# Message passing with 42-node ranges, batches added in pairs per PSUM bank, one-hots three batches ahead, and VectorE's batch work all ahead of the reset gate

## The reference, cut to what matters

```python
def _gated_graph_conv(x, src, dst, emask, W, wih, whh, bih, bhh):
    h = x
    for i in range(STEPS):                      # 3 steps, and this for each of 3 edge types
        m = h @ W[i]
        msg = m[src] * emask[:, None]
        agg = jax.ops.segment_sum(msg, dst, num_segments=N)
        h = _gru_cell(agg, h, wih, whh, bih, bhh)
    return h
...
dst = (3125 * uniform(50000) ** 2.0).astype(int32); sorted   # dense at low nodes, thin at high ones
```

## Time and profile before

| what | us |
|---|---|
| median of 3 runs | 2778.94 (2778.64 to 2779.45) |
| the profiled execution: span from first to last instruction | 3036.4 |
| three steps of the graph convolution in it (601 to 2500) | 1899 |
| everything ahead of them (mix stage) | 601 |
| everything behind them (expert stage) | 536 |

### The profile page before, as it was taken

One profiled execution on the slowest core, in us unless ns is written; L12 is line 12 of the kernel. 1 busy time (PEld: TensorE's weight loads), 2 busy tenths in 40 slices (PEclk: granted clock), 3 DMA queues, 4 the chain that ended last, 5 costly groups with the idle time before them and its releaser, 6 DMA issues. The chain is left out here.

```text
span 3036.4 us, 39301 instructions
## 1 busy us (share of the span) xinstructions
PE 2646.3 (87%) x13041; PEld 1701.2 (56%) x13041; DVE 1592.0 (52%) x3119; ACT 642.5 (21%) x1180; POOL 1358.7 (45%) x1375
## 2 busy tenths in 40 slices
PE   5898899779988898798899996898888966999997
PEld 3434455465555556554455554654545556788886
DVE  6798777445555554355555552466766784011110
ACT  3211000111111114111111123122212221332232
POOL 0000500066666661666666634666666600333333
PEclk7899999889999999899999998899999985999998
DMA  4300766334444443444444434343444423133223
GB/s 129 132 1 1 286 240 218 117 104 129 144 144 137 138 135 104 126 125 145 128 129 145 145 97 157 118 121 112 123 129 124 122 58 100 35 90 92 65 64 72
DMA packets 201473, 362.85 MB, mean 120 GB/s; under 512 B 27937, under 2 KB 156109, under 8 KB 201104
## 3 DMA queue, kind: packets, MB, share of 16 engines
q0 software_dynamic: 67776, 169.95, 20.2%
q1 hardware_dynamic: 129564, 186.48, 18.4%
q10 hardware_dynamic: 3956, 4.19, 0.5%
HBM read 293.37 MB, written 70.34 MB: 120 GB/s over the span
## 5 line engine op out<-in xcount | busy, mean ns | idle before, releaser
L1453 POOL DMA_INDIRECT xnT<-h_rows,idx x780 | 775.2, 994 | 378.0 <-issue 206.6
L1124 PEld LDWEIGHTS g_pagg<-g_onehot,xnT 128*128 128x128 f16 x4680 | 337.1, 99 | 408.3 <-issue 396.3
L1124 PE MATMUL g_pagg<-g_onehot,xnT 128*128 128x144 f16 x4680 | 416.0, 230 | 154.8 <-issue 152.8
L1295 DVE TENSOR_TENSOR g_agg<-g_agg,g_pagg 128x288 f32 x585 | 265.1, 453 | 370.6 <-remote 159.6
L1453 POOL DMA_INDIRECT xnT<-xn_rows,idx x366 | 360.6, 985 | 198.8 <-issue 95.0
L1298 DVE SCALAR_TENSOR_TENSOR g_onehot<-iota_keys,shift,keys 128x288 f16<-128x288 f16 x585 | 299.1, 513 | 0.6 <-DVE g_pre_at L1287 0.3
L1201 PE MATMUL g_pr<-g_agg,g_wc 128*128 128x448 f32 (+1 forms) x576 | 231.1, 520 | 18.1 <-DVE g_agg L1295 9.1
L1387 DVE SCALAR_TENSOR_TENSOR g_t<-g_ph,g_bh,g_rT 128x448 f32<-128x448 f32 (+1 forms) x144 | 89.8, 624 | 282.3 <-remote 199.1
L1201 PE MATMUL g_pz<-g_hT,g_wh 128*128 128x448 f32 (+1 forms) x576 | 224.4, 509 | 9.9 <-issue 5.9
L1201 PE MATMUL g_pz<-g_agg,g_wc 128*128 128x448 f32 (+1 forms) x576 | 228.8, 520 | 1.1 <-issue 0.9
L1201 PE MATMUL g_pr<-g_hT,g_wh 128*128 128x448 f32 (+1 forms) x576 | 224.8, 512 | 3.7 <-issue 3.5
(11 more groups left out here) (356 smaller groups left out, 3371.7 us busy)
## 6 DMA issues: line engine op xcount, KB each, us to landing
ma_R<-q_cols SPq DMA_DIRECT2D x27, 896.0 KB, 12.0
f_w<-in_L_ffn_W SPq DMA_DIRECT2D x16, 1024.0 KB, 7.7
h_cols<-g_hn SPq DMA_DIRECT2D x36, 448.0 KB
h_rows<-g_rows SPq DMA_DIRECT2D x36, 448.0 KB
g_hT<-h_cols SPq DMA_DIRECT2D x36, 448.0 KB
mix_R<-q_cols SPq DMA_DIRECT2D x15, 896.0 KB, 9.6
xnT<-h_rows,idx POOLq DMA_INDIRECT x780
ma_R<-q_cols SPq DMA_DIRECT2D x9, 1120.0 KB, 5.9
```

What stands on the lines that cost most here:

```text
L1124: mm = e.matmul(pg[:, k * TYPES:(k + 1) * TYPES, :].rearrange("p t d -> p (t d)"), rows[:, c, o:o + P], hot[:, c, :], start=(c == 0 and pa ...
L1295: e.tensor_tensor(agg[:, :, bass.ds(o, DT)], agg[:, :, bass.ds(o, DT)], pagg[b % BANKS][:, :, :], ALU.add).then_inc(S["added"], 1)
L1453: e.indirect_dma_start(ring[:, b % SLABS, c, :], None, tables[s], bass.IndirectOffsetOnAxis(ap=idx[:, o:o + 1], axis=0)).then_inc(landed[b ...
```

## The change

The ranges shrink from 48 to 42 nodes, and the sums of two batches lie in one PSUM bank (2 x 6 x 42 = 504 of the 512 fp32 that the kernel's widest PSUM tensors have): the 3 banks hold 6 batches. Since two batches share a bank, VectorE adds the two only when both are counted, and TensorE begins a bank again only when both of its batches are added. One-hots are made three batches ahead instead of one, in a ring of 7 instead of 4. Four batches instead of three may be outstanding when a group starts (KEPT), which moves the plan by one batch. In VectorE's order the slots 5 and 6 come ahead of the reset gate.

```diff
-DT = 48
+DT = 42
-BANKS, KEPT, SURE = 3, 3, 1
+BANKS, HALVES, KEPT, SURE = 3, 2, 4, 1
+SUMS = BANKS * HALVES
+AHEAD, HOTS = 3, 7
...
+def added_by(b):
+
+    if b == MB - 1:
+        return MB
+    whole = PLAN[0] // HALVES * HALVES if b >= PLAN[0] - 1 else 0
+    return max(0, b // HALVES * HALVES - HALVES, whole)
...
-    return MB if g == NG - 1 else PLAN[GPU * NU * g] - (KEPT if g else 0)
+    return MB if g == NG - 1 else added_by(PLAN[GPU * NU * g] - 1)
...
-        onehot = sb("onehot", [P, 4, BATCH, NKEY], F16)
+        onehot = sb("onehot", [P, HOTS, BATCH, NKEY], F16)
...
-        pagg = [ps(f"pagg{i}", [P, KC * TYPES, DT]) for i in range(BANKS)]
+        pbank = [ps(f"pagg{i}", [P, HALVES, KC * TYPES, DT]) for i in range(BANKS)]
+        pagg = [pbank[i // HALVES][:, i % HALVES, :, :] for i in range(SUMS)]
...
-                if b >= BANKS:
-                    e.wait_ge(S["added"], s * MB + b - BANKS + 1)
+                if b >= SUMS and b % HALVES == 0:
+                    e.wait_ge(S["added"], s * MB + b - SUMS + HALVES)
...
-            e.wait_ge(S["batch"], s * MB + b + 1)
+            e.wait_ge(S["batch"], s * MB + min(MB, b // HALVES * HALVES + HALVES))
...
         def dve_batches(e, s, p):
             for b in range(batches_before(p - 1), batches_before(p)):
-                if b >= BANKS and not PLAN[0] <= b < PLAN[0] + BANKS:
-                    dve_add(e, s, b - BANKS)
+                for i in range(added_by(b - 1), added_by(b)):
+                    dve_add(e, s, i)
                 if b == 0:
-                    dve_onehot(e, s, 0)
-                if b + 1 < MB:
-                    dve_onehot(e, s, b + 1)
-                if b in (PLAN[0] - 1, MB - 1):
-                    for i in range(BANKS):
-                        dve_add(e, s, b - BANKS + 1 + i)
+                    for i in range(AHEAD):
+                        dve_onehot(e, s, i)
+                if b + AHEAD < MB:
+                    dve_onehot(e, s, b + AHEAD)
...
                         if v < UNITS:
-                            dve_reset_gate(e, s, v)
                             dve_batches(e, s, GPU * v + 5)
                             dve_batches(e, s, GPU * v + 6)
+                            dve_reset_gate(e, s, v)
                             dve_candidate(e, s, v)
```

More of the change, by code:

```diff
@@ L296, in dve_edges @@
             step(e.tensor_copy(most_i[:, :], most[:, 0:1]))
-            step(e.tensor_scalar(most_i[:, :], most_i[:, :], 4, None, ALU.logical_shift_right))
-            step(e.tensor_scalar(most_i[:, :], most_i[:, :], 171, None, ALU.mult))
-            step(e.tensor_scalar(most_i[:, :], most_i[:, :], 9, None, ALU.logical_shift_right))
+            step(e.tensor_scalar(most_i[:, :], most_i[:, :], 1, None, ALU.logical_shift_right))
+            step(e.tensor_scalar(most_i[:, :], most_i[:, :], 3121, None, ALU.mult))
+            step(e.tensor_scalar(most_i[:, :], most_i[:, :], 16, None, ALU.logical_shift_right))
             step(e.tensor_copy(most[:, 1:2], most_i[:, :]))
@@ L1175, in pe_range @@
                 e.wait_ge(S["onehot"], s * MB + b + 1)
-                if b >= BANKS:
-                    e.wait_ge(S["added"], s * MB + b - BANKS + 1)
+                if b >= SUMS and b % HALVES == 0:
+                    e.wait_ge(S["added"], s * MB + b - SUMS + HALVES)
                 e.wait_ge(landed[b % SLABS], landings(s, b))
-                count_batch(e, pagg[b % BANKS], ring[:, b % SLABS, :, :], onehot[:, b % 4, :, :], S["batch"])
+                count_batch(e, pagg[b % SUMS], ring[:, b % SLABS, :, :], onehot[:, b % HOTS, :, :], S["batch"])
         def pe_unit(e, s, v):
@@ L1282, in dve_pre @@
                     e.wait_ge(V[s]["batch"], r * NB + b + 1)
-                    e.tensor_tensor(agg[:, :, bass.ds(o, DT)], agg[:, :, bass.ds(o, DT)], pagg[0][:, :, :], ALU.add).then_inc(V[s]["added"], 1)
+                    e.tensor_tensor(agg[:, :, bass.ds(o, DT)], agg[:, :, bass.ds(o, DT)], pagg[0], ALU.add).then_inc(V[s]["added"], 1)
                     e.wait_ge(V[s]["added"], r * NB + b + 1)
@@ L1291, in dve_add @@
             o = e.value_load(main_at[0:1, b + 1:b + 2], min_val=0, max_val=NP)
-            e.wait_ge(S["batch"], s * MB + b + 1)
+            e.wait_ge(S["batch"], s * MB + min(MB, b // HALVES * HALVES + HALVES))
             if b:
                 e.wait_ge(S["added"], s * MB + b)
-            e.tensor_tensor(agg[:, :, bass.ds(o, DT)], agg[:, :, bass.ds(o, DT)], pagg[b % BANKS][:, :, :], ALU.add).then_inc(S["added"], 1)
+            e.tensor_tensor(agg[:, :, bass.ds(o, DT)], agg[:, :, bass.ds(o, DT)], pagg[b % SUMS], ALU.add).then_inc(S["added"], 1)
         def dve_onehot(e, s, b):
-            e.scalar_tensor_tensor(out=onehot[:, b % 4, :, :], in0=iota_keys[:, :].unsqueeze(1).to_broadcast([P, BATCH, NKEY]), scalar=shift[:, 0:1],
+            e.scalar_tensor_tensor(out=onehot[:, b % HOTS, :, :], in0=iota_keys[:, :].unsqueeze(1).to_broadcast([P, BATCH, NKEY]), scalar=shift[:, 0:1],
                                    in1=keys[:, BATCH * (b + 1):BATCH * (b + 2)].unsqueeze(2).to_broadcast([P, BATCH, NKEY]), op0=ALU.add, op1=ALU.is_equal).then_inc(S["onehot"], 1)
```

## The result

The changed kernel takes 2805.23 us (2803.10 to 2809.38, 4 runs), the kernel before 2779.19 beside it: a ratio of 1.0096 (95% interval 1.0083 to 1.0108), so it is 1% slower, 26.7 us. The prediction was 2745 with a range of 2705 to 2778: the sign is wrong, and the time lies outside the range.

A forecast was written before the change was run, and what follows sets the result against it. It took TensorE, busy 87% of the span, as the bound, with GpSimd's gathers as a 533 us floor in steps 1 and 2. Step 0 gained 22 us, steps 1 and 2 7 and 5: 2779 - 34 = 2745 us, range 2705 to 2778.

The forecast's parts named there:

- The profiled execution against the runs: Profiled span 257 us above the median run; taken off the three steps, leaving about 547 us each, 20 for waits.
- Adds in pairs: VectorE adds two batches together, with the same number of adds and register loads; claimed effect zero.
- GpSimd's floor: Gathers and pauses of 489 us, plus 2.5 and 41, keep steps 1 and 2 from going below 533 us.
- the gathers' floor is reached already: Rival: unprofiled steps 1 and 2 already go at GpSimd's pace, only step 0 gains 12 to 22; 2762 us, chance 0.13.
- Columns: Counting matmuls go from 144 to 126 columns: 7.5 ns each, 35 us; the skill's second formula agrees, its 81 ns doesn't.
- the rival of the weight load: Weight load sets the counting matmuls' pitch at 0.062 us, so the 35 us fall away; 2753 to 2783, chance 0.10.
- Waits for an add: TensorE's waits for VectorE's adds ahead of counting matmuls, 89 us profiled; priced at 10 us saved per step in runs.
- waits real in the runs: Rival: nearly all 89 us of waits for adds exist in unprofiled runs too; about 2690 us, chance 0.20.
- VectorE's shorter operations: 36 columns less save 37 ns on each of 1170 VectorE instructions, 43 us, hidden behind TensorE.
- Plan: Second group begins behind 28 batches instead of 27; +2 us each in steps 1 and 2, nothing in step 0.
- Reset gate behind the slots: VectorE's reset gate comes after slots 5 and 6; t1 up to two slots later, candidate hardly; claimed effect zero.
- The slower rival: The later reset gate delays z, each of 108 wide units losing perhaps 0.4 us; +43 - 20, 2800 us, chance 0.11.

The follow-up runs named there:

- e6_one_add_a_slot: The changed kernel with one add in each slot instead of two in every second; 2778.85 us, ratio 1.0002 to the kernel before.

## Why the prediction was wrong, point by point

The loss is the sum of three measured parts: columns -5.8 us, adds in pairs +26, plan +7.5. That is +27.7 for the 26.7 measured. The parts are the steps of one chain of kernels (columns alone, one add a slot with KEPT = 3, one add a slot, changed), so the sum has to close but for the step from the first to the second (0.9979 to 0.9975, -1 us), which holds the banks in pairs, the one-hots three ahead and the reset gate's place: nothing beyond the noise.

- **The profiled execution against the runs.** Half right. Taking the 257 us off the three steps gave 547 us a step, and on the usual chip the three take 2774.2 - 599.6 - 529.3 = 1645, which is 548 each. But I kept 20 us per step of it for TensorE's waits, from a trace in which matmuls that wait for nothing stand apart; on the usual chip these waits aren't there. The spans, 2774.2 for an execution of 2775.88 and 3029.9 for one of 3031.66, show that the kind of chip and not the profiling makes the difference. So the forecast span of 2930 has no meaning on the usual chip.
- **Adds in pairs: "Zero."** This is the step that turned the sign. It looked at what a pair does to TensorE's waits (rightly nothing: 1.3 us of idle time behind an add) and not at what VectorE's order does to GpSimd. It costs 26 us, through gathers that are 24.4 us longer (`e6_one_add_a_slot` against the changed kernel). In the difference of the two traces only 17 us of it show, probably because shorter operations gave some 7 back: in the trace with the columns alone the gathers are 7.4 us shorter.
- **GpSimd's floor.** Mis-sized, and by its own rows. The 489 us add to 390 gathers only those pauses that the profile puts on "issue", 103.3 us for 339 gathers; the other 51 have the same 0.3 us inside a longer wait. All 390 at 0.990 + 0.30 make 503, and 503 + 2.5 + 41 = 547 is the very length that the prediction gave a step: no room was left, not 14 us. Steps 1 and 2 of the kernel before take 505.5 and 511.9 us of gathers on the usual chip, at 992 and 1009 ns each with no wait for the ring worth naming: at the floor. The rival "the gathers' floor is reached already" had the right state of the kernel, at a chance of 0.13, but its 2762 let step 0 gain, and the gathers set the pace there as well (473.7 us for 366).
- **Columns.** The pitch was right: eight matmuls take 0.60 us for 0.66, (0.60 - 0.22)/7 = 0.054 apart, so the second formula of the Trainium skill holds here (55 ns) and the 81 ns don't; the rival of the weight load falls. The worth was wrong: not 35 us but 5.8, since TensorE doesn't bound. Even these may come from gathers held for less by shorter one-hots (7.4 us in one trace); that isn't shown.
- **Waits for an add.** -30 was forecast, about 0 is there: in the kernel before on the usual chip the named waits ahead of counting matmuls make 38.9 of 39.3 us, and none is for an add. In the trace that the prediction read they were real (154.8 us ahead of counting matmuls, 89 for adds), but not in the runs whose time was asked for. The rival "waits real in the runs" falls too.
- **VectorE's shorter operations.** Sizes as forecast: adds 453 to 417 ns, one-hots 513 to 475. "Hidden behind TensorE" wasn't the point: one-hots made far shorter (242 ns) take 34 us off the gathers.
- **Plan.** +4 was forecast, 7.5 measured. The last batch in the fourth slot of unit 41 and not the sixth leaves two slots' more gate work behind it at each of three ends (43.8, 44.1, 61.5 for 40.8, 41.3, 56.9); I had priced only the second group's start and left the ends out. In the timeline the last batch now stands ahead of pi's matmuls, where in the kernel before it stands ahead of z's second set. KEPT = 3 in the changed kernel brings the ends back to 41.1, 41.1 and 56.8.
- **Reset gate behind the slots: zero.** Right: 1.0100 with it first, 1.0096 with it last. The slower rival was wrong in its mechanism; that its sign and its time (2800) came near is luck.

## What to carry to other kernels

When the profiled execution and the runs differ by 9%, don't price waits from that trace: it may be another chip, and then its waits are not those of the kernel that is timed. Ask first which engine never stops; here it was GpSimd, busy only 49% of the span and some 70% of a step but pausing only its fixed 0.3 us between gathers. Add that pause to every gather when you work out a floor, not only to those whose idle time has the label. An order of instructions that is neutral for its own engine and for whoever waits for it can still slow a third engine through what they share: in this kernel an indirect DMA of GpSimd that starts inside a VectorE operation on SBUF alone is held until it ends. So look at what is under way when each gather starts, not at busy shares, and time any order that bunches such operations; here one add that reads PSUM to each one-hot was the best tried.

## What was not expected of the hardware

- An indirect DMA of GpSimd for 128 rows occupies it for some 955 ns, and up to 2.27 us in the changed kernel when it starts beside VectorE's work on SBUF: it then ends 0.825 us after that work does. Summed over 1146 gathers the excess over 957 is 29 us (one-hots of 14 columns), 39 (columns alone; one add a slot), 46 (before) and 63 (after).
- The kernel before takes 2779 to 2781 us on three chips of these runs, and 3038 and 3059 on two others. On the latter the gathers are as long (998 ns), but matmuls and waits show gaps of several tenths of a us and more; why is open.
